# Splitting the later keys and values into products of 128 columns, and handing half of the preparation's key stores to GpSimd

## The reference, cut to what matters

```
x = x + tanh(g_xattn[0]) * L0_xattn(layernorm(x), ctx, ctx, Wq, bq, Wk, bk, Wv, bv, Wo, bo)
x = x + tanh(g_ffn[0])   * L0_ffn(layernorm(x), ...)
...                                  # L1, L2, L3 in the same way
qh = split_heads(q @ Wq + bq);  kh = split_heads(k @ Wk + bk);  vh = split_heads(v @ Wv + bv)
scores = einsum('bhqd,bhkd->bhqk', qh, kh) / sqrt(8)
out = einsum('bhqk,bhkd->bhqd', softmax(scores), vh) @ Wo + bo
```

## Time and profile before

| | us |
|---|---|
| median of three runs | 3122.69 (3119.62 to 3124.01) |
| the profiled execution | 3128.37, its span 3126.4 |
| preparation, to the first scores | 0 to 117.0 |
| four sweeps of L0 | 117 to 504 |
| mean granted TensorE clock | 0.982 |

### The profile page before, as it was taken

One profiled execution on the slowest core, in us unless ns is written; L12 is line 12 of the kernel. 1 busy time (PEld: TensorE's weight loads), 2 busy tenths in 40 slices (PEclk: granted clock), 3 DMA queues, 4 the chain that ended last, 5 costly groups with the idle time before them and its releaser, 6 DMA issues.

```text
span 3126.4 us, 54830 instructions
## 1 busy us (share of the span) xinstructions
PE 3009.3 (96%) x18636; PEld 1138.3 (36%) x18636; DVE 494.3 (16%) x1341; ACT 2522.6 (81%) x2892; POOL 205.8 (7%) x732
## 2 busy tenths in 40 slices
PE   5899999999989799999999999899899999999999
PEld 3333333323333523333333334666522222322256
DVE  2310010000122501100111013644300000100012
ACT  2699999999933299999999997322399999999963
POOL 3000000000000000000000001100000000000000
PEclk9899999999989999999999999999899999999999
DMA  6222121111240012112211124010011111111110
GB/s 161 65 63 74 47 68 52 37 37 57 62 105 0 14 53 64 60 58 73 66 37 39 53 66 124 21 46 1 3 37 37 37 37 46 54 38 36 37 39 8
DMA packets 166931, 157.25 MB, mean 50 GB/s; under 512 B 20776, under 2 KB 121628, under 8 KB 166748
## 3 DMA queue, kind: packets, MB, share of 16 engines
q1 hardware_dynamic: 159776, 149.27, 16.0%
q0 software_dynamic: 1088, 3.34, 0.3%
q10 hardware_dynamic: 5884, 2.08, 0.3%
HBM read 121.89 MB, written 32.91 MB: 50 GB/s over the span
## 4 chain that ended last, share of the span: by engine, by line
PE 92%; DVE 4%; issue 1%; SPq 1%; ACT 1%; POOL 1%; DMA 0%; ACTq 0%; DVEq 0%; POOLq 0%
PE PS L2243 40%; PE PS L2262 31%; PE PS L754 5%; PE PS L739 5%; PE PS L741 2%; PE PS L1050 2%; PE PS L1036 1%; PE PS L1513 1%; PE PS L1510 1%; SPq L1591 1%; PE PS L1037 0%; PE PS L1085 0%; PE PS L2223 0%; PE PS L2156 0%; PE PS L2229 0%
## 5 line engine op out<-in xcount | busy, mean ns | idle before, releaser
L2018 ACT ACTIVATE probs<-PS 128x1024 f32<-128x1024 f32 x2496 | 2283.2, 1234 | 41.7 <-PE PS L2262 36.7
L2243 PE MATMUL PS<-probs,vr 128*32 128x512 f32 (+1 forms) x9984 | 1327.4, 604 | 1.9 <-DVE accs L2488 1.9
L2262 PE MATMUL PS<-qs,kr 35*128 35x512 f32 (+2 forms) x4992 | 1067.2, 482 | 8.8 <-ACT probs L2018 3.4
L2262 PEld LDWEIGHTS PS<-qs,kr 35*128 35x128 f32 x4992 | 449.1, 184 | 1187.3 <-ACT probs L2018 819.1
L1849 POOL COPY vr<-vs 128x72 f32 (+1 forms) x624 | 157.8, 253 | 2694.6 <-PE PS L2243 2473.8
L777 ACT ACTIVATE probs<-PS 128x512 f32<-128x512 f32 x192 | 114.5, 598 | 272.0 <-PE PS L739 143.9
L2243 PEld LDWEIGHTS PS<-probs,vr 128*32 128x32 f32 x9984 | 197.3, 108 | 339.5 <-issue 272.2
L754 PEld LDWEIGHTS PS<-wide,probs 128*128 128x128 f32 x1280 | 151.5, 194 | 17.5 <-issue 16.7
L754 PE MATMUL PS<-wide,probs 128*128 128x128 f32 x1280 | 153.8, 277 | 0.5 <-DVE kf L812 0.5
L2488 DVE COPY accs<-PS 128x512 f32<-128x512 f32 x12 | 8.3, 692 | 782.8 <-PE PS L2229 782.8
L739 PE MATMUL PS<-xT,wide 128*128 128x512 f32 x224 | 106.7, 594 | 1.0 <-DVE probs L796 1.0
(11 more groups left out here) (313 smaller groups left out, 1203.2 us busy)
## 6 DMA issues: line engine op xcount, KB each, us to landing
kr<-key_pieces SPq DMA_DIRECT2D x1248, 64.0 KB
key_pieces<-kparts SPq DMA_DIRECT2D x172, 96.0 KB, 2.8
kr<-mask_strips SPq DMA_DIRECT2D x624, 4.0 KB
values<-kf SPq DMA_DIRECT2D x34, 216.0 KB, 4.1
vs<-values SPq DMA_DIRECT2D x2, 3672.0 KB, 16.9
c_T<-turned_context SPq DMA_DIRECT2D x18, 192.0 KB, 4.1
key_pieces<-probs SPq DMA_DIRECT2D x32, 96.0 KB, 3.2
c_in<-turned_context SPq DMA_DIRECT2D x16, 192.0 KB, 4.2
```

Of the source, the lines that this page charges most:

```text
L2018: sc.activation(prob[n % RING][:, :, q0:], PS[:, bank:bank + 2, q0:], ACT.Exp, scale=SCALE).then_inc(p_ready, 1)
L2243: last = te.matmul(PS[32 * j:32 * j + 32, 7, q0:], vr[s.buf(c)][:, at_v:at_v + 32], prob[(n + j // 2) % RING][:, j % 2, q0:], start=fresh, ...
L2262: last = te.matmul(o, kr[b][own, p, :], qs[own, T8 // 2 * s.hh + p, 512 * s.qh + q0:512 * s.qh + 512], start=True, stop=True)
```

## The change

There are two parts.

**Preparation.** The two stores of the low key part go from SyncE's queue to GpSimd's, behind the store of the turned tile, and all three count on one semaphore, `pool_out`. The squares have two buffers and are taken from the high key part in SBUF, behind the copy of the next turned tile. The high part signals by itself (`k_high`), so that SyncE's stores and VectorE's low part no longer wait for the squares. TensorE's keys of a tile wait for the low part of two tiles before and no longer of the tile before. ScalarE's copy of the next turned tile now waits until all three GpSimd stores of two tiles before it have landed, where it waited for the one.

**Sweeps.** A later item of keys is three products of 128 columns in place of one of 384, and keys and values are issued product by product: with one such item in a round, behind every second group; with two, behind every group.

```diff
-        def later_pe(pe, a, q):
+        def later_pe(pe, a, q, c):
...
-            if n:
+            if n and c == 0:
                 pe.wait_ge(v_ev, NTILE + n)
+            turned = ct_later[j % 2][:, c * P:c * P + P]
             if kind == "keys":
-                pe.wait_ge(c_loaded[j % 2], 16 * (PREP_LOADS[j % 2] + use + 1))
-                last = te.matmul(PS[:, 6, 0:TW], wk[:, a, :], ct_later[j % 2], start=True, stop=True)
+                if c == 0:
+                    pe.wait_ge(c_loaded[j % 2], 16 * (PREP_LOADS[j % 2] + use + 1))
+                last = te.matmul(PS[:, 6, c * P:c * P + P], wk[:, a, :], turned, start=True, stop=True)
             elif kind == "values":
-                for c in range(TC):
-                    last = te.matmul(PS[:, 6, c * P:c * P + P], ct_later[j % 2][:, c * P:c * P + P], wv5[:, a, :], start=True, stop=True)
+                last = te.matmul(PS[:, 6, c * P:c * P + P], turned, wv5[:, a, :], start=True, stop=True)
...
-                            items = later_items(s.w, i)
+                            pieces = [(n, q, c) for n, q in later_items(s.w, i) for c in range(1 if LATER_ITEMS[q][0] == "norms" else TC)]
                             for c in range(TC):
                                 for g in range(2):
                                     scores(i * TC + c, g)
                                     values(s, i * TC + c - 1, g)
-                                if c < len(items):
-                                    later_pe(pe, *items[c])
+                                    for k, piece in enumerate(pieces):
+                                        if k * 2 * TC // len(pieces) == 2 * c + g:
+                                            later_pe(pe, *piece)
```

The preparation, on SyncE, GpSimd, ScalarE, TensorE and VectorE in this order:

```diff
+        def store_keys(eng, j, off, e, c):
+            return eng.dma_start(key_scr[bass.ds(at(j, off, TC, 0), TC), 0, e, c].rearrange("c d t k -> (d t) c k"),
+                                 kparts2[off % 2][HALF * e:HALF * e + HALF, c, :, 0, :].bitcast(F32))
...
-                for c, done in enumerate((k_act, k_low)):
-                    sp.wait_ge(done, at(j, off, 1, 1))
-                    for e in range(2):
-                        sp.dma_start(...).then_inc(k_out[b], 16)
-                    if ahead and c == 0:
-                        sp.wait_ge(gram_mm, at(j, off, 1, 1))
-                        load_ctx(j, off + UNROLL, ahead)
+                sp.wait_ge(k_high, at(j, off, 1, 1))
+                for e in range(2):
+                    store_keys(sp, j, off, e, 0).then_inc(k_out[b], 16)
+                if ahead:
+                    sp.wait_ge(gram_mm, at(j, off, 1, 1))
+                    load_ctx(j, off + UNROLL, ahead)
...
-                g.dma_start(ct_scr[...], c_T[off % 2]).then_inc(ct_out[off % 2], 16)
+                g.dma_start(ct_scr[...], c_T[off % 2]).then_inc(pool_out[off % 2], 16)
+                pool.wait_ge(k_low, at(j, off, 1, 1))
+                for e in range(2):
+                    store_keys(g, j, off, e, 1).then_inc(pool_out[off % 2], 16)
...
-                buffer_out(act, k_out, STORES, j, off)
+                buffer_out(act, k_out, HIGH_STORES, j, off)
                 act.wait_ge(k_ps, at(j, off, 1, 1))
-                if not first:
-                    act.wait_ge(kn_ps, at(j, off, 1, 0))
...
-                sc.activation(ksq[:, 0, :], keys, ACT.Square, bias=bqk[:, 1, 0:1]).then_inc(k_act, 1)
                 if not last:
                     rows(j, off + 1, first)
+                if not first:
+                    act.wait_ge(kn_ps, at(j, off, 1, -1))
+                act.wait_ge(k_high, at(j, off, 1, 1))
+                sc.activation(ksq[:, b, :]..., kparts2[b][:, 0, :, 0, :].bitcast(F32), ACT.Square).then_inc(k_act, 1)
             def rows(j, off, first=False):
...
-                    buffer_out(act, ct_out, 16, j, off)
+                    buffer_out(act, pool_out, POOL_STORES, j, off)
...
-                    pe.wait_ge(k_low, at(j, off, 1, 0))
+                    pe.wait_ge(k_low, at(j, off, 1, -1))
...
-                buffer_out(dve, k_out, STORES, j, off)
-                dve.wait_ge(k_act, at(j, off, 1, 1))
+                buffer_out(dve, pool_out, POOL_STORES, j, off)
+                dve.wait_ge(k_high, at(j, off, 1, 1))
```

More of the change, by code:

```diff
@@ L256, in flamingo_decoder @@
         kn_ev = sem("kn_ev")
-        ct_out = [sem(f"ct_out{b}") for b in range(2)]
+        pool_out = [sem(f"pool_out{b}") for b in range(2)]
+        k_high = sem("k_high")
         later_k_out = [sem(f"later_k_out{b}") for b in range(2)]
@@ L1491, in flamingo_decoder @@
         KEYS_OUT = [STORES * u for u in USES]
+        HIGH_STORES = 16 * 2
+        HIGH_OUT = [HIGH_STORES * u for u in USES]
+        POOL_STORES = 16 * 3
+        POOL_OUT = [POOL_STORES * u for u in USES]
         ROUNDS = (NTILE - 1) // UNROLL - 1
@@ L1516, in later_pe @@
                 last = te.matmul(PS[32 * a:32 * a + 32, 6, 0:TW], head_of[:, :], ksq[:, 0, :], start=True, stop=True)
-            last.then_inc(gram_mm, 1)
+            if kind == "norms" or c == TC - 1:
+                last.then_inc(gram_mm, 1)
         def later_dve(dve, chain, a, q):
@@ L1634, in _ @@
                 for b in range(2):
-                    sp.wait_ge(k_out[b], KEYS_OUT[b] + (STORES if a > 1 else 0))
+                    sp.wait_ge(k_out[b], HIGH_OUT[b] + (STORES if a > 1 else 0))
+                    sp.wait_ge(pool_out[b], POOL_OUT[b])
                     if a:
@@ L1686, in _ @@
                         for b in range(2):
-                            sp.wait_ge(ct_out[b], 16 * USES[b])
+                            sp.wait_ge(pool_out[b], POOL_OUT[b])
                     else:
@@ L1829, in k_step @@
                 pool.wait_ge(ct_ready, at(j, off, 1, 1))
-                g.dma_start(ct_scr[bass.ds(at(j, off, 1, 0), 1), :, :].rearrange("o p k -> p (o k)"), c_T[off % 2]).then_inc(ct_out[off % 2], 16)
+                g.dma_start(ct_scr[bass.ds(at(j, off, 1, 0), 1), :, :].rearrange("o p k -> p (o k)"), c_T[off % 2]).then_inc(pool_out[off % 2], 16)
+                pool.wait_ge(k_low, at(j, off, 1, 1))
+                for e in range(2):
+                    store_keys(g, j, off, e, 1).then_inc(pool_out[off % 2], 16)
             k_step(None, 0)
@@ L1879, in k_step @@
                 b = off % 2
-                buffer_out(act, k_out, STORES, j, off)
+                buffer_out(act, k_out, HIGH_STORES, j, off)
                 act.wait_ge(k_ps, at(j, off, 1, 1))
-                if not first:
-                    act.wait_ge(kn_ps, at(j, off, 1, 0))
                 keys = PS[:, 1 + b, 0:TW]
-                sc.activation(kparts2[b][:, 0, :, 0, :], keys.rearrange("p (c k) -> p c k", c=TC), ACT.Identity, bias=bqk[:, 1, 0:1])
-                sc.activation(ksq[:, 0, :], keys, ACT.Square, bias=bqk[:, 1, 0:1]).then_inc(k_act, 1)
+                sc.activation(kparts2[b][:, 0, :, 0, :], keys.rearrange("p (c k) -> p c k", c=TC), ACT.Identity, bias=bqk[:, 1, 0:1]).then_inc(k_high, 1)
                 if not last:
                     rows(j, off + 1, first)
+                if not first:
+                    act.wait_ge(kn_ps, at(j, off, 1, -1))
+                act.wait_ge(k_high, at(j, off, 1, 1))
+                sc.activation(ksq[:, b, :].rearrange("p (c k) -> p c k", c=TC), kparts2[b][:, 0, :, 0, :].bitcast(F32), ACT.Square).then_inc(k_act, 1)
             def rows(j, off, first=False):
@@ L1981, in _ @@
                             for b in range(2):
-                                act.wait_ge(k_out[b], KEYS_OUT[b])
+                                act.wait_ge(k_out[b], HIGH_OUT[b])
+                                act.wait_ge(pool_out[b], POOL_OUT[b])
                                 act.wait_ge(later_k_out[b], KEYS_OUT[b])
@@ L1989, in _ @@
                         if a == 0 and i == 0:
-                            act.wait_ge(ct_out[1], 16 * USES[1])
+                            act.wait_ge(pool_out[1], POOL_OUT[1])
                         sc.activation(q_parts[:, 0, cols(i)], PS[:, 2 + i, :], ACT.Identity, bias=bqk[:, 0, a:a + 1])
@@ L2071, in norms @@
                     pe.wait_ge(kn_ev, at(j, off, 1, 0))
-                te.matmul(PS[0:32, 7, 0:TW], head_of[:, :], ksq[:, 0, :], start=True, stop=True).then_inc(kn_ps, 1)
+                te.matmul(PS[0:32, 7, 0:TW], head_of[:, :], ksq[:, off % 2, :], start=True, stop=True).then_inc(kn_ps, 1)
             def k_step(j, off, first=False, last=False, before_last=False):
@@ L2381, in _ @@
                             for b in range(2):
-                                dve.wait_ge(k_out[b], KEYS_OUT[b])
+                                dve.wait_ge(k_out[b], HIGH_OUT[b])
+                                dve.wait_ge(pool_out[b], POOL_OUT[b])
                                 dve.wait_ge(later_k_out[b], KEYS_OUT[b])
```

8 lines of the change are left out of this document (3 added, 5 removed).

## The result

The changed kernel takes 3138.73 us in the median of 20 runs (3122.5 to 3168.8); the kernel before, beside it, 3123.62 (3119.62 to 3128.66). The ratio is 1.0052, with a 95% interval of 1.0034 to 1.0069: slower by half a per cent, where I had forecast 3105. The spread matters as much as the median: 9 us before, 46 us after. The mean granted TensorE clock goes with it: 0.982 in the run of 3122.5 us, 0.976 at 3139.8, 0.965 at 3168.8.

The account below looks back on a forecast made before the run. ScalarE was taken to set the sweeps' pace, with TensorE stalls at items. 3128.4 - 19.5 (sweeps) + 2 (preparation) = 3110.9 us profiled; with the runs' median 5.7 below, 3105, range 3093 to 3118.

Parts of the forecast that it names:

- What bounds the kernel: Sweeps: ScalarE sets the pace at 1.84 us per group; TensorE could do 1.66, a slack of 0.18.
- The sweeps at full clock: Sweeps: stalls at later items fall from 20.6 us to 1.1, giving back 19.5.
- the lone product: Sweeps, TensorE: a single product of 128 columns between groups costs 0.29 us, at most 0.55.
- My own threshold: Sweeps: two groups give TensorE back 2 x 0.18 = 0.36 us; a dearer product is no longer recovered.
- The second sweep: Sign of being right: ScalarE's blocks merge at 0.917 to 0.92 per exponential, and this sweep is 3.3 us shorter.
- Rival 1: Sweeps: lone products cost more; at 0.45, 3123 to 3125; at 0.55, 3143, chance 0.02. At 0.40 to 0.45, shares 0.13.
- a round of six products: Sweeps: six products in six groups leave TensorE 0.84 us late, 0.27 over; four such rounds cost 1.1 together.
- VectorE ... has over a round until SyncE stores it: Sweeps: VectorE gets items up to 4 groups later, with time to spare before SyncE's store; cost put at 0.
- The two-tile loop: Preparation: ScalarE's copy waits for GpSimd's low stores of two tiles before; 8.5 us, 4.27 per tile against 4.29 now.
- my bounds of -4 to +9: Preparation: start and end together +2 us, from -4 (landings of 2.5) to +9 (3.6, issue 0.85).
- rivals, 1 and 2: The second: preparation, GpSimd slow at key stores; 6.4 us per tile gives 3134, chance 0.05; 4.8 to 5.6 shares 0.13.
- slower 0.07: Whole kernel: chance of a time above 3129 us; faster had 0.80, same 0.13.

Follow-up runs that it names:

- e7: Changed kernel with SyncE's stores of a sweep's last items moved behind the next loads of keys; 3127.8 us, ratio 1.0024 to the kernel before.
- e2: Kernel before with the change's sweeps part alone (split products), preparation as before; 3130.4 us, ratio 1.0017.
- e4: e2 with SyncE's store of a sweep's last-round item behind the next load of keys but one; 3117.7 us, ratio 0.9981.
- e5: Kernel before, nothing split, last-round item of a sweep moved behind the first group of the round's last chunk; 3128.2 us, ratio 1.0013.
- e6: As e5, with the last-round item one group later still; 3137.3 us, ratio 1.0040 to the kernel before.
- e3: The changed kernel run again, unchanged; 3147.2 us, ratio 1.0064 to the kernel before.
- e8: e2 with the pieces of a sweep's last round behind its last groups, differing from e6 in splitting alone; 3137.3 us, ratio 1.0052.
- e9: e7 with ScalarE's copy waiting only for the turned tile's store, as before; low stores stay on GpSimd; 3106.1 us, ratio 0.9958.
- e10: e9 with the low stores back on SyncE, behind the load; 3111.0 us, ratio 0.9968 to the kernel before.
- e12: Kernel before with items split apart only in rounds 1 to 3 of the first sweeps of L0 and L1; 3124.6 us, ratio 1.0022.
- e13: e9 with products alone behind three groups in a row in rounds 1 to 3 of L0's and L1's first sweeps; 3111.9 us, ratio 0.9968.
- e1: Changed kernel with the later items as before, so the preparation's part alone; 3135.9 us, ratio 1.0040 to the kernel before.
- e11: e9 with an item's products together in rounds 1 to 3 of the first sweeps of L0 and L1; 3107.9 us, ratio 0.9946.
- e15: e11 with the items of two-item rounds whole as well; 3107.1 us, ratio 0.9949 to the kernel before.
- e14: e11's kernel run once more, beside e15 on one chip; 3107.8 us, ratio 0.9947 to the kernel before.

## Why the prediction was wrong

**What bounds the kernel: right at full clock.** There ScalarE sets the pace at 0.917 in every sweep, and TensorE's slack is 0.18 per group. At half clock TensorE does, at 3.01 per group.

**The sweeps at full clock: mechanism right, size wrong.** I took 0.29 for the lone product, with bounds 0.29 to 0.55; it is 0.42. My own threshold was 0.36, above which TensorE no longer gets back what a product takes. Adding up by how much the distances between exponentials exceed 0.917 in the six sweeps with items (behind their first twelve exponentials), it was 23.0 us before and is 15.0 after: 8.0 given back, or 9.6 without the late keys at 1283.50 and 1481.70, and not 19.5. The second sweep is 1.1 us shorter, not 3.3. Rival 1 had the right mechanism; three products at 0.42 bring 1.26 against 1.08, so an item still costs 0.18 where it cost 0.29, and 68 x 0.11 = 7.5. And a round of six products costs 1.2 of stalls, where I had 1.1 for all four such rounds.

**"VectorE ... has over a round until SyncE stores it": a term put at 0 that isn't.** It is true in the middle of a sweep and false for its last round, whose items SyncE stores at once, ahead of the next keys. I named the wait and did not ask for the last round. Moving these stores and nothing else takes 11 to 19 us off the median of the changed kernel (e7) and 12.7 off e2's (e4), and e5 and e6 bracket the price from the side of the kernel before, at 4.5 and 13.6. It comes off as fewer longer runs: 29 of 51 in the split kernels with the stores as they were (changed, e2, e3, e8), 11 of 48 with the stores moved (e4, e7, e9, e10).

**No step for the clock: the other failure.** I counted every product at its full-clock price, although the trace of before has the clock at half for the first 20.5 us of the first sweep, some 12 us ahead of the earlier trace rows. With a first item in lone products such a start can last 60 us, at some 20 us each. Longer runs, and not a cost that every execution has, make a median 16 us above the profiled run. How the 16 us divide between late keys and these starts is not settled. My range of 3093 to 3118 was worked out from one execution at one clock. That such starts are among the changed kernel's longer runs is inferred: both profiles of it were of short runs, and the long stretches are seen in e9, e10, e12 and e13, which have the same lone products. Open stays how late keys and the clock work together: e4 has far fewer longer runs than e2 (1 and 6 of 12), so falls behind late keys may also last longer with lone products, but no profile caught one; e8's, of 13.7 us at 1479.3, is the nearest, and e6 has 10.2 with whole items.

**The preparation: mechanism right, three terms too small.** The two-tile loop is what binds: each copy starts 0.10 behind the landing of GpSimd's second low store of two tiles before, in nearly every tile. I put it at 8.5 for two tiles; from the copy at 32.27 (tile 2) to the one of tile 14 at 91.14 it is 58.87 / 6 = 9.81. By terms, one loop, from the timeline of all engines:

```profile
71.70 0.49 ACT L1911 ACTIVATE c_T<-PS 128x384 f32<-128x384 f32 x1 [1.80 <-DMA key_pieces<-kparts]
...
72.24 0.91 PE L2095 MATMUL PS<-c_T,wk 128*128 128x384 f32 x2 [1.10 <-ACT c_T L1911]
...
74.86 0.58 ACT L1897 ACTIVATE kparts<-PS,bqk 128x384 fp32r<-128x384 f32 x1 [2.26 <-issue]
...
75.71 0.60 DVE L2345 SCALAR_TENSOR_TENSOR kparts<-PS,bqk,kparts 128x384 fp32r<-128x384 f32 x1
...
76.98 1.28 POOL L1568 DMA_DIRECT2D key_pieces<-kparts  x2 [2.24 <-DVE kparts L2345]
...
81.80 0.49 ACT L1911 ACTIVATE c_T<-PS 128x384 f32<-128x384 f32 x1 [3.08 <-DMA key_pieces<-kparts]
```

From the keys to the end of the low part it is 4.07 here (forecast 4.03) and 4.61 in the mean of the six loops; the longest, 6.0, was at half clock. From the end of the low part, 76.31, to GpSimd's issue it is 0.67, where I put 0.1. The issue is 0.64 (0.6), and the second store lands 4.08 behind its own, 3.24 in the mean (3.1). So +0.58 for the keys, +0.57 for the handover and +0.14 for the landing make up the 1.3. That made the preparation +6.4 in the profiled run, inside my bounds of -4 to +9, against +2; in the runs of e1 it is +12. e7 against e9 says what the wait itself costs, since without it the other edits of this part gain: 22 us. I took the loop of 4.27 to be as good as the 4.29 it replaced, and never asked what the kernel would do without it.

**Landings by queue.** In the changed kernel's preparation GpSimd's key stores land in 2.4 and 2.9 us in the median and SyncE's in 3.1 and 2.3, by buffer. The Trainium skill, DMA: Bandwidth & Descriptors, section Latency and other measured facts, has the first byte at about 1 us from GpSimd and 0.6 from SyncE; the landings of this trace don't show such a difference. What is late on GpSimd is the start of the issue.

**The chances.** I gave slower 0.07. Of my rivals, 1 and 2 both came halfway, each at a price that I had within its bounds, and together they cancel my gain; the longer runs then made it slower.

## What to carry to other kernels

Where TensorE starts a stage at its low clock, keep the few large products whole, and split them only once the clock is up, as e11 does; compare runs by their granted clock before believing one profile. When an item is spread over a loop's body, check the last turn of the loop, and what stands behind it in the queue of whoever waits for it. A semaphore that joins a slow store to a fast one makes every waiter wait for the slower: count them apart.

## What the runs showed of the hardware

- At 1.2 GHz with TensorE busy nearly throughout (56.97 of 57 us in e10), the granted clock stayed low for up to 61 us on scores and values with lone 128 x 128 products between them. It rose 1.6 to 2.0 us after the start of a whole product of 384 columns in the six cases in which one found it low (e6, e10 twice, e11, e13, e15), and twice behind lone products only (e9, e12).
- A lone fp32 product of 128 columns between fp32r scores and values costs 0.42 us, three in a row 0.86, at 2.4 GHz; at 1.2 GHz a lone one costs 0.72 (124.58 to 125.30) and three in a row 1.58 (1099.02 to 1100.60).
- A wait of TensorE of 2.1 to 2.7 us in the middle of full work was followed by 3.4 to 13.7 us at half clock (e6 and e8, two each); waits of 1.29 and 1.54 (e4, e3) by 3.4; e6's of 1.05 and the changed kernel's four of 0.5 to 1.0 by none. The length of the wait doesn't decide alone: behind e14's of 0.43 stand 17.1 us.
- GpSimd began a key store 0.67 to 0.70 us behind the end of VectorE's low part inside its loop, and 0.30 behind it in the unrolled tiles after the loop.
